# Two of the third group's four tiles give up their lower kinds in the third and fourth head too

## The reference

```
z = einsum('ni,hoi->hno', h, W)              # h is the layer-normed input
e = leaky_relu(e_src[src] + e_dst[dst], 0.01)
alpha = softmax of e over the edges of one destination
out[dst] = sum over edges of alpha * z[src]  # per head
x = x + out
```

## Time and profile before

| what | value |
|---|---|
| runs before | 1694.79 to 1695.71 us, median 1695.35 |
| profiled execution, its own time | 1694.51 us |
| span of the profile | 1692.8 us |
| granted clock of TensorE, mean | 0.98 |
| busy over the span | PE 1547.1 us (91%), weight loads 1354.6 (80%), DVE 1031.5 (61%), ACT 1030.3 (61%) |
| the stage's matmuls | from 271.7 us to 741.2 us of the span |

### The profile page before, as it was taken

One profiled execution on the slowest core, in us unless ns is written; L12 is line 12 of the kernel. 1 busy time (PEld: TensorE's weight loads), 2 busy tenths in 40 slices (PEclk: granted clock), 3 DMA queues, 4 the chain that ended last, 5 costly groups with the idle time before them and its releaser, 6 DMA issues. The chain is left out here.

```text
span 1692.8 us, 33810 instructions
## 1 busy us (share of the span) xinstructions
PE 1547.1 (91%) x11582; PEld 1354.6 (80%) x11582; DVE 1031.5 (61%) x1831; ACT 1030.3 (61%) x1884; POOL 82.6 (5%) x117
## 2 busy tenths in 40 slices
PE   5788886999999999989998999999999999999696
PEld 4577766999999999966665999977799998776465
DVE  6799995899999999974454221132421222876661
ACT  2566675888889898853433656556565555566220
POOL 3000000000000000020000100000000000120213
PEclk9899998999999999989999999999999999999799
DMA  7335640644736555027660545445454444666211
GB/s 215 98 92 142 155 118 29 158 109 96 157 74 136 107 104 112 1 70 145 142 139 9 127 111 127 114 127 133 129 141 119 125 109 117 162 151 154 65 48 39
DMA packets 236969, 190.60 MB, mean 113 GB/s; under 512 B 107274, under 2 KB 231624, under 8 KB 236848
## 3 DMA queue, kind: packets, MB, share of 16 engines
q1 hardware_dynamic: 226938, 176.22, 43.4%
q0 software_dynamic: 6368, 9.36, 2.2%
q10 hardware_dynamic: 3542, 3.46, 0.8%
HBM read 114.58 MB, written 53.86 MB: 100 GB/s over the span
## 5 line engine op out<-in xcount | busy, mean ns | idle before, releaser
L1662 PE MATMUL ps_sets<-arena,kinds_mem 125*125 125x195 bf16 (+1 forms) x2500 | 445.7, 250 | 28.3 <-DVE kinds_mem L1403 18.6
L1387 ACT ACTIVATE kinds_mem<-ed_rows,es_mask 125x625 bf16<-125x625 f32 x500 | 366.5, 809 | 61.7 <-PE ps_sets L1668 34.0
L1668 PE MATMUL ps_sets<-arena,kinds_mem 125*125 125x195 bf16 (+1 forms) x2300 | 394.8, 249 | 0.0
L1662 PEld LDWEIGHTS ps_sets<-arena,kinds_mem 125*125 125x125 bf16 x2500 | 343.1, 137 | 36.4 <-DVE kinds_mem L1403 25.6
L2863 ACT ACTIVATE onewide<-ring 125x625 fp32r (+1 forms) x325 | 222.5, 720 | 168.6 <-PE oneps L2580 95.3
L1668 PEld LDWEIGHTS ps_sets<-arena,kinds_mem 125*125 125x125 bf16 x2300 | 315.5, 137 | 0.0
L2552 PE MATMUL oneps<-onewide,parts_a 125*128 125x376 f32 (+1 forms) x2000 | 293.0, 308 | 8.0 <-DVEq L2643 8.0
L2552 PEld LDWEIGHTS oneps<-onewide,parts_a 125*128 125x128 f32 x2000 | 291.2, 190 | 8.9 <-DVEq L2641 8.4
L2580 PE MATMUL oneps<-oneparts_b,onewide 125*125 125x512 f32 x1000 | 234.6, 395 | 0.0
L2580 PEld LDWEIGHTS oneps<-oneparts_b,onewide 125*125 125x125 f32 x1000 | 184.5, 185 | 48.6 <-DVE onefull L2715 1.9
L1395 DVE TENSOR_TENSOR kinds_mem<-kinds_mem,blk 125x2500 bf16<-125x2500 bf16 x120 | 182.3, 1520 | 40.5 <-ACT kinds_mem L1387 31.4
(11 more groups left out here) (447 smaller groups left out, 1823.9 us busy)
## 6 DMA issues: line engine op xcount, KB each, us to landing
ring<-counts SPq DMA_DIRECT2D x50, 683.6 KB
ring<-countsT SPq DMA_DIRECT2D x40, 683.6 KB
countsT<-cut_mem SPq DMA_DIRECT2D x107, 136.7 KB
blk<-counts SPq DMA_DIRECT2D x20, 546.9 KB
counts<-blk SPq DMA_DIRECT2D x3, 3418.0 KB
counts<-kinds_mem SPq DMA_DIRECT2D x2, 3418.0 KB
ed_rows<-ed_dram SPq DMA_DIRECT2D x16, 273.4 KB
ring<-countsT SPq DMA_DIRECT2D x10, 410.2 KB
```

Source lines behind the costliest of these rows:

```text
L1387: return k.nc.scalar.activation(kinds_of(k)[:, slot, 0, :], k.ed_b[:, h, :], ACT.Relu, scale=MASK_SCALE, bias=k.es_mask[:, t, h:h + 1])
L1662: t_.matmul(out[0], kind[0], z[0], start=(t == 0), stop=False)
L1668: last = t_.matmul(out[1], kind[1], z[1], start=False, stop=(t == T - 1))
```

## The change

The pair of heads becomes a number of tiles per head. Heads 0 and 1 keep all four tiles of group 2 in the three-matmul form; heads 2 and 3 now have two tiles of four in it. `lower_kinds` gets a `skip`: in heads 2 and 3 it works on two tiles of group 2 (1250 elements per partition in place of 2500). PE issues 5 more matmuls with their weight loads for each tile so treated. Because PE now reads `cnt` in the last head too, SP waits for PE's end of group 2 before it loads the next block's counts of that group.

```diff
-def lower_kinds(k, m):
+def lower_kinds(k, m, skip=0):
...
-    return k.nc.vector.tensor_tensor(out=kinds[:, lo:hi, 1, :], in0=k.blk[:, t0:t0 + n, :], in1=kinds[:, lo:hi, 0, :], op=ALU.subtract)
+    return k.nc.vector.tensor_tensor(out=kinds[:, lo + skip:hi, 1, :], in0=k.blk[:, t0 + skip:t0 + n, :], in1=kinds[:, lo + skip:hi, 0, :],
+                                     op=ALU.subtract)
...
-    WHOLE_HEADS = (0, 1)
+    WHOLE_TILES = (4, 4, 2, 2)
...
                         sp.wait_ge(kinds_done, T * (HEADS * b - 1) + sum(GROUPS[m]))
+                        if m == WHOLE:
+
+                            sp.wait_ge(group_done, (NM - 1) * HEADS * b + m + 1)
                         load_cnt(b - 1, m)
...
-                    if m == WHOLE and h in WHOLE_HEADS:
+                    skip = WHOLE_TILES[h] if m == WHOLE else 0
+                    if skip == n:
                         above.then_inc(kinds_done, n)
                         return
                     v.drain()
-                    lower_kinds(k, m).then_inc(kinds_done, n)
+                    lower_kinds(k, m, skip).then_inc(kinds_done, n)
...
-                                        if m == WHOLE and h in WHOLE_HEADS:
+                                        if m == WHOLE and s < WHOLE_TILES[h]:
```

## The result

| | kernel before | changed kernel | ratio, 95% interval |
|---|---|---|---|
| first timing, 22 runs each | median 1696.22 us | median 1700.05 us | 1.0020 (1.0012 to 1.0027) |
| profiled span | 1692.8 us | 1697.9 us | |

The change made the kernel slower, clear of noise and just at the 0.2% that the prediction set as its bound. The median met the forecast of 1700.2 partly by luck: in these runs the kernel before stood at 1696.2, not 1695.35, so the difference is 3.8 us where 4.84 was forecast.

A forecast was written before the change was run, and what follows sets the result against it. Heads 2 and 3 were taken as bound by the 7.76 us turnaround to group 5; 1.21 + 0.84 + 3 × 0.93 = 4.84 us on the median 1695.35 gave 1700.2 us, with an eight-in-ten range of 1697.2 to 1702.8.

The forecast's parts named there:

- What bounds the heads: Heads 2 and 3: a fixed turnaround of 7.76 us from group 2's last matmul to group 5 sets the pace.
- the ring: Slots' path from PE's end of group 2 over ACT's masks and DVE's kinds to PE's group 5, 7.76 us.
- DVE's half lower kinds: Group 2 in ten heads: 1250 elements take about 0.80 us, saving 0.66 us each, 6.6 in all.
- The added matmuls: PE's group 2: 10 more matmuls a head at 84.2 ns, 0.84 us a head, 8.4 in all.
- the rival of slower pairs: Added matmul pairs on PE take up to 137 ns, up to 5.3 us more in all; chance 0.05.
- The sum: Heads 2 and 3 of five blocks: two heads take 45.76 us, the whole 4.84 us longer.
- Nothing takes the delay up: Head 0 of the next block passes the delay through undiminished; the rival that it absorbs it had chance 0.10.
- SP's wait costs nothing: Next block's counts of group 2 load later but 15 us before DVE wants them; rival of late counts, chance 0.02.
- The size in the timing: Whole run: 1700.2 us beside the median, +0.29%; under 0.2% can't be told from none.

The follow-up runs named there:

- The split: Changed kernel, with DVE making group 5's kinds in two parts in heads 2 and 3: ratio 0.9964; the same edit on the kernel before: 0.9997.
- its own kernel: Kernel before with only SP's new wait for PE's group 2 before loading the next block's counts: ratio 1.0004.
- four tiles: Changed kernel with all four tiles of group 2 in the three-matmul form in every head: 1708.92 us, one execution.
- the split in the first block: Changed kernel with group 5's kinds made in two parts in heads 2 and 3, and in the first block's heads 0 and 1 too: ratio 0.9965.

## Why the prediction was right

- *What bounds the heads.* Right. The turnaround from group 2's last matmul to group 5 was 7.76 to 7.77 us in heads 2 and 3 of the kernel before, of the changed one and of every kernel that left the ring alone and its work in group 2. The split, which shortens it, turned the loss into a gain, and left these heads of the kernel before at 22.42 us; that shows the cause.
- *DVE's half lower kinds.* Read from the line through two sizes as 0.80 us; measured 0.81.
- *The added matmuls.* Right at 84 ns; the rival of slower pairs fell. From two tiles to four, 10 more matmuls a head cost 23.73 − 22.88 = 0.85 us, 85 ns each. The rule that the prediction took from the Trainium skill, "TensorE: Matmul & The Clock Gate", section "LDWEIGHTS (loading the stationary operand)", a load of columns divided by 1.2 in ns, makes an estimate of 104 ns for 125 columns if loads set the pace. The traces disagree in these 85 ns.
- *The sum.* 4.84 us forecast, 4.90 in the stage, of it 4.88 in heads 2 and 3. Head 22.88 forecast and measured, ACT's wait 1.27 forecast and measured.
- *Nothing takes the delay up.* Right: from the fourth head's group 5 to the next block's first it is 24.74 to 24.80 us in both kernels, the same in each block within 0.01.
- *SP's wait costs nothing.* Right, by its own kernel.
- *The size in the timing.* The timings gave 0.20% and 0.25%, not 0.29%. Part may be noise (the kernel against itself gave 0.03% ± 0.1%). Part may be the stage's entry, described in the last section. The runs don't settle it.

## What to carry to other kernels

This rests on one kernel. When engines hand slots round a ring, measure the turnaround from the release of a slot to the first use of its next content, and compare it with the work the consumer has in between. Where the turnaround is the longer of the two, work moved to the consumer ahead of the release lengthens the loop in full, even where the consumer had waits: they are the rest of the turnaround and only move. Work moved inside the turnaround, or a turnaround cut in parts, is what turns such a trade into a gain; try both edits together, as each alone may show nothing.

## What was not expected of the hardware

The stage's first matmuls run slowly after PE has been idle for 8.4 us, and the length of this entry varied by 2.5 us between profiles. The window from 272 to 284 us, kernel before and then changed, columns as in the earlier trace rows:

```profile
272.00:284.00 12.00, 11.18 (x96) 10.88 (x95) 2.91 (x2) 5.33 (x8) 0.00 (x0) 0.70 0.01 3
```

```profile
272.00:284.00 12.00, 11.30 (x111) 11.03 (x112) 4.48 (x5) 7.55 (x12) 0.00 (x0) 0.81 0.01 4
```

The granted clock is 0.70 and 0.81 of 2.4 GHz: part of it at 1.2 GHz, with 163 ns from matmul to matmul, and then at 2.4 GHz with 84 ns. From the stage's first matmul to the first of group 2 it took 10.98 us in the profile before and 11.37 in that kernel's second one, but 9.14 and 9.10 in two of the changed kernel. Over all 13 profiles, seven took 10.6 to 11.4 us and six 8.9 to 9.5. After the fourteenth matmul each has a pause in which PE waits for nothing that the profile shows; start to start it is 0.90 to 1.30 us in the seven and 0.63 to 0.76 in the six. That makes up the smaller part of the difference. The larger is how many matmuls ran at the lower level before the clock rose, 39 to 46 in the seven and 21 to 28 in the six. What decides it stays open. All five profiles with the kernel before's matmuls are among the seven, but so are two with more matmuls (four tiles, and the split in the first block). So the changed kernel may gain 1.9 us of its 4.9 back at the entry, which would fit the timings. That is an association in few profiles and no experiment tested it.
